# Three graph hops: relation rows from one fp32 one-hot matmul per half group in place of two bf16 ones

## The chip, the core and the metric

One core of one Trainium2 chip. The metric is the device time in microseconds of one execution of the whole program, from one launch; lower is better.

## What is computed

Two graph layers on 6250 nodes with 128 features and 206250 edges (100000 drawn edges, their reverses and one loop per node). The first is an attention layer with two heads. The second, around which the change lies, makes three hops, each over all edges; an edge has one of 64 relations, whose embedding row multiplies the row of its tail node:

```python
head, tail = edge_index            # 206250 edges
rel = edge_emb[edge_type]          # 64 x 128 table, one row per edge
for _ in range(3):
    h, t = agg[head], agg[tail]
    left = h @ q_w
    right = jnp.tanh(rel * t @ k_w)
    att = jnp.sum(left * right, axis=1)
    e = jnp.exp(att - seg_max[head])
    w = e / seg_sum[head]
    summed = segment_sum(w[:, None] * rel * t, head)
    agg = summed / max(cnt, 1);  agg = agg / max(norm(agg), 1e-12)
    out = out + agg + entity_emb
```

## The kernel before

The kernel first sorts the edges by node (until about 830 us of the profile), then runs the attention layer as a pipeline over groups, then the three hops, each again such a pipeline with some bookkeeping between them. A group is 256 edges (`G`), held as two halves of 128. There are 854 groups (`NG`), taken as 61 bodies of 14 (`U`), so the three hops make 2562 groups. The last groups of a pass stand at the end of the sorted list.

There is no scheduler: `pipeline` (line 112) calls one step function per engine and group number k, and in step k each engine works on groups j = k minus a fixed lag, in the written order. Semaphores join the engines. For a hop, the work of one group is:

- POOL (GpSimd), line 705: two indirect DMAs that gather the 128 tail rows of each half into `rows_r`, a ring of 7 groups (`R`). Ahead of them it waits until the group seven back has been multiplied (`val_done`) and its row numbers have been loaded (`peers`).
- SP: once in 7 groups (a unit) it loads for the next unit the target keys (`key_d`, line 461), the small per-group numbers (`meta_d`) and the relation numbers (`type_d`, line 464), keys and relation numbers broadcast to the partitions; for every group the 64 KB tile of `left_d` (line 476); and it stores the finished states (line 483).
- DVE, `masks` (line 1494, lag 4): the one-hot of the relations `hot_r` (line 1503), then the mask of the keys `off_r` (line 1504). At lag 5 line 1655 multiplies the gathered rows with the relation rows out of `bank[0]` into `val_r`. At lag 8 line 1648 takes the running minimum of the scores, and lines 1630 and 1632 accumulate at lag 12.
- PE, in the order of a step: the weighted sums (line 876, lag 11), the transposes of the probabilities (line 882, lag 10), the scores (line 888), the product with `k_w` (line 892), the transposes of `val_r` (line 897, lag 6), and last the relation rows (lines 904 and 905, lag 5). All calls of the helper `mm` show as L737, so its tiles tell them apart: `emb_pair` and `emb_low` for the relation rows, `arena` alone with 128x129 for the sums, `wide` for the scores, `kw_s` for the product.
- ACT: the exponentials (line 1081, lag 9), a count (line 1084), the fade factor (line 1086), and three evacuations of PSUM: line 1090 (probabilities), line 1094 (tanh), line 1098 (`valT`, lag 6).

The relation rows are made exact in bf16 by splitting the fp32 embedding into three bf16 parts. `type_r` holds the relation numbers on all 128 partitions, so `hot_r` has 128 rows: rows 0 to 63 and 64 to 127 are the same one-hot, by `rel_row`. `emb_pair` stacks the high and middle parts, and one matmul over 128 rows adds both; a second, over 64 rows, adds `emb_low`. The parts are prepared once, by nine DVE instructions in `pack` at n == 14, in the sort.

Of the kernel before, what the change touches and what calls it, by code (L numbers as in the profile page):

```python
# [5 lines left out]
P = 128  # L6
N = 6250
E = 206250
F = 128
# [11 lines left out]
R = 7  # L21
# [104 lines left out]
def gnn_kernel(nc, x, src, dst, etype, w, attn_l, attn_r, bias, gamma, beta, emb, q_w, k_w, out):  # L126
    with ExitStack() as ctx:
        ctx.enter_context(nc.allow_non_contiguous_dma(reason="narrow columns of edges and scores"))

        def sb(name, shape, dt=F32):  # L130
            return ctx.enter_context(nc.sbuf_tensor(name, shape, dt))
# [46 lines left out]
        emb_s = sb("emb_s", [2 * RELS, F])  # L178
        emb_rest = sb("emb_rest", [2 * RELS, F])
        emb_high = sb("emb_high", [2 * RELS, F], BF16)  # L180
        emb_pair = sb("emb_pair", [2 * RELS, F], BF16)
        emb_low = sb("emb_low", [RELS, F], BF16)
        rel_row = sb("rel_row", [2 * RELS, 1])
# [95 lines left out]
        hot_r = ring((R, G), BF16)  # L279
# [116 lines left out]
        def _(sp):  # L396
# [18 lines left out]
            for a, d in ((qw_s[:], q_w), (kw_s[:], k_w), (emb_s[0:RELS], emb), (emb_s[RELS:2 * RELS], emb)):  # L415
                sp.dma_start(a, d).then_inc(late_in, 16)
# [21 lines left out]
            def load_store(layer):  # L438
                q = pipes[layer]

                def step(b, k):
# [9 lines left out]
                    if not b.last and k % R == 0 and not (layer == 1 and b.first and k == 0):  # L451
# [11 lines left out]
                        if layer == 1:  # L463
                            sp.dma_start(flat(type_r), row(type_d).partition_broadcast(P)).then_inc(d, 16)
# [21 lines left out]
            def first_unit():  # L486
# [5 lines left out]
                sp.dma_start(flat(type_r), type_d[0:R * G].partition_broadcast(P)).then_inc(d, 16)  # L492
# [242 lines left out]
        def _(pe):  # L735
# [131 lines left out]
            def hop_pe_step(b, k):  # L867
# [32 lines left out]
                if b.has(j):  # L900

                    pe.wait_ge(q["off_done"], b.count(j))
                    for c in range(2):
                        mm(bank[0][:, c * P:(c + 1) * P], hot_r[:, j % R, c * P:(c + 1) * P], emb_pair[:], True, False)
                        last = mm(bank[0][:, c * P:(c + 1) * P], hot_r[0:RELS, j % R, c * P:(c + 1) * P], emb_low[:], False, True)
# [228 lines left out]
        def _(dve):  # L1134
# [79 lines left out]
            def pack(n):  # L1214

                if n == 2:
                    dve.wait_ge(late_in, 10 * 16)
# [15 lines left out]
                elif n == 14:  # L1233
                    do(V.tensor_copy(emb_high[:], emb_s[:]))
                    do(V.tensor_tensor(emb_rest[:], emb_s[:], emb_high[:], ALU.subtract))
                    do(V.tensor_copy(emb_pair[0:RELS], emb_high[0:RELS]))
                    do(V.tensor_copy(emb_pair[RELS:2 * RELS], emb_rest[RELS:2 * RELS]))
                    do(V.tensor_copy(emb_high[0:RELS], emb_rest[0:RELS]))
                    do(V.tensor_tensor(emb_s[0:RELS], emb_rest[0:RELS], emb_high[0:RELS], ALU.subtract))
                    do(V.tensor_copy(emb_low[:], emb_s[0:RELS]))  # L1240
# [490 lines left out]
```

## Time and profile before

| | |
|---|---|
| median of 3 runs | 9809.54 us (9796.19 to 9809.73) |
| the profiled execution, its own time | 9807.02 us |
| span of its trace | 9805.2 us |
| mean granted TensorE clock | 0.979 |
| sort | to about 830 us |
| attention pass, first to last gather | about 830 to 2970 us |
| hop 1, 2, 3: first gather at | 3094, 5332, 7565 us |
| busy share of PE, DVE, ACT, POOL | 91%, 81%, 75%, 69% |

The profile comes from one execution. Engines run side by side, and a busy share is a mean over stages. PE rows give matmuls and PEld rows their weight loads; a matmul overlaps the next one, so the pace of a chain of them is the distance between the starts and not their durations. An fp32 matmul of the program stands as two instructions in the trace, each with a weight load. Time in which an engine waits for nothing that the profile shows is called issue.

### The profile page before, as it was taken

Reading aid. Unit: us, or ns where it says so; the run is one execution under the profiler, and the core shown is the slowest. Engines: PE = TensorE matmul, PEld = TensorE weight load, DVE = VectorE, ACT = ScalarE, POOL = GpSimd, SP = SyncE. Lnnn points to the kernel's source line nnn. Section 1 sums busy time; section 2 is a strip of 40 time slices with the busy share of each in tenths; the row PEclk is TensorE's granted clock in tenths of the full one; section 3 lists DMA queues with packets and bytes.
Section 4 is the critical chain, followed back from the end, with each engine's and each line's share of the span. In section 5 each row is a group of like instructions: output and inputs, shape, how many; then the busy total and the mean of one; then the engine's idle time right before and its main releaser. Section 6 shows DMA issues by size and latency. Waiting matters only on the chain.

```text
span 9805.2 us, 277571 instructions
## 1 busy us (share of the span) xinstructions
PE 8923.7 (91%) x65693; PEld 7235.6 (74%) x65693; DVE 7921.7 (81%) x33650; ACT 7321.4 (75%) x23591; POOL 6810.7 (69%) x7059
## 2 busy tenths in 40 slices
PE   7996777777776999999997999999997999999997
PEld 6985666666664777777775777777775777777775
DVE  7898999999997777777775777777775777777775
ACT  2204999999996777777775777777775777777775
POOL 1336777777775777777775777777775777777775
PEclk9998999999997999999998999999998999999998
DMA  2003444444444555555556555555556555555556
GB/s 49 5 12 82 108 109 109 109 109 109 109 109 115 159 159 159 159 159 158 159 159 133 158 160 160 157 159 159 159 159 140 159 159 159 159 159 159 159 159 122
DMA packets 1133743, 1308.57 MB, mean 133 GB/s; under 512 B 452629, under 2 KB 847723, under 8 KB 1133325
## 3 DMA queue, kind: packets, MB, share of 16 engines
q1 hardware_dynamic: 899446, 841.26, 28.0%
q0 software_dynamic: 229008, 460.45, 21.1%
q10 hardware_dynamic: 5126, 4.76, 0.2%
q8 instruction: 94, 1.54, 0.1%
q14 instruction: 69, 0.56, 0.0%
HBM read 1041.61 MB, written 260.45 MB: 133 GB/s over the span
## 4 chain that ended last, share of the span: by engine, by line
PE 63%; DMA 10%; DVE 9%; issue 8%; POOL 7%; ACT 3%; SPq 1%; DVEq 0%; POOLq 0%; ACTq 0%
PE bank L737 52%; DMA agg<-agg_d,arena 6%; POOL agg L705 6%; PE bank L897 5%; PE bank L882 5%; PE bank L850 2%; DMA agg<-feat_d,arena 2%; DVE agg L1545 2%; DVE agg L1555 2%; ACT arena L1011 2%; DVE arena L1535 1%; POOL wide L718 1%; DMA arena<-type_d 1%; DVE arena L1513 1%; DVE arena L1504 0%
## 5 line engine op out<-in xcount | busy, mean ns | idle before, releaser
L705 POOL DMA_INDIRECT agg<-agg_d,arena x5124 | 4852.1, 947 | 1731.1 <-issue 1432.1
L1655 DVE TENSOR_TENSOR arena<-agg,bank 128x256 f32<-128x256 f32 x2562 | 1080.2, 422 | 1451.1 <-PE bank L737 1064.4
L705 POOL DMA_INDIRECT agg<-feat_d,arena x1708 | 1618.3, 947 | 529.4 <-issue 421.4
L737 PE MATMUL bank<-arena 128*128 128x129 f32 x10248 | 1825.6, 300 | 32.6 <-ACT arena L1090 30.5
L737 PE MATMUL bank<-tmp,wide 128*128 128x256 f32 x5124 | 1540.1, 383 | 10.1 <-DMA wide<-left_d 10.1
L737 PE MATMUL bank<-tmp,kw_s 128*128 128x256 f32 x5124 | 1532.9, 381 | 0.0
L737 PEld LDWEIGHTS bank<-arena 128*128 128x128 f32 x10248 | 1338.5, 190 | 211.3 <-issue 43.3
L1086 ACT ACTIVATE arena<-arena 128x1 f32<-128x1 f32 x2562 | 754.6, 295 | 931.7 <-DVE arena L1519 890.6
L1081 ACT ACTIVATE arena<-agg,arena 128x256 f32<-128x256 f32 x2562 | 1337.9, 522 | 57.8 <-DVE arena L1648 52.2
L1094 ACT ACTIVATE tmp<-bank 128x256 f32<-128x256 f32 x2562 | 982.1, 383 | 427.6 <-PE bank L737 372.6
L1648 DVE CUSTOM_DVE_ANT_0 agg<-bank,arena 128x256 f32<-128x256 f32 x2562 | 1228.6, 480 | 19.6 <-issue 8.0
L737 PE MATMUL bank<-emb_low,arena 64*128 64x128 bf16 x5124 | 1160.3, 226 | 0.0
L737 PE MATMUL bank<-emb_pair,arena 128*128 128x128 bf16 x5124 | 1153.0, 225 | 1.8 <-ACT wide L1002 1.8
L737 PEld LDWEIGHTS bank<-tmp,kw_s 128*128 128x128 f32 x5124 | 979.0, 191 | 134.1
L897 PE MATMUL bank<-ident,arena 128*128 128x128 f32 x5124 | 989.3, 275 | 82.4 <-DVE arena L1655 80.4
L1084 ACT ACTIVATE tmp<-arena 128x256 bf16<-128x256 bf16 x2562 | 1059.9, 414 | 0.0
L1504 DVE TENSOR_SCALAR arena<-arena 128x256 bf16<-128x256 uint16 x3416 | 999.7, 293 | 0.0
L897 PEld LDWEIGHTS bank<-ident,arena 128*128 128x128 f32 x5124 | 715.0, 141 | 373.6 <-DVE arena L1655 125.5
L882 PE MATMUL bank<-ident,arena 128*128 128x128 f32 x5124 | 981.2, 273 | 0.0
L1098 ACT COPY tmp<-bank 128x256 f32<-128x256 f32 x2562 | 942.4, 368 | 17.9 <-PE bank L897 17.5
L850 PE MATMUL bank<-ident,arena 128*128 128x128 f32 x3416 | 561.6, 287 | 425.1 <-ACT arena L1011 423.3
L1513 DVE TENSOR_SCALAR arena<-arena 128x1 f32<-128x1 f32 (+1 forms) x3416 | 930.1, 272 | 0.0
(242 smaller groups left out, 17251.0 us busy)
## 6 DMA issues: line engine op xcount, KB each, us to landing
state_d<-arena SPq DMA_DIRECT2D x488, 455.0 KB, 2.7
arena<-key_d SPq DMA_DIRECT2D x489, 448.0 KB
arena<-type_d SPq DMA_DIRECT2D x367, 448.0 KB
wide<-left_d SPq DMA_DIRECT2D x2562, 64.0 KB
agg<-agg_d,arena POOLq DMA_INDIRECT x5124
agg<-feat_d,arena POOLq DMA_INDIRECT x1708
arena<-er_d SPq DMA_DIRECT2D x854, 1.0 KB
arena<-peers SPq DMA_DIRECT2D x489, 7.0 KB
```

What stands on the lines that cost most here:

```text
L705: nc.gpsimd.indirect_dma_start(out=rows_r[:, k % R, c, 0:width], out_offset=None, in_=table, in_offset=bass.IndirectOffsetOnAxis(ap=peer_r ...
L737: return nc.tensor.matmul(out, lhsT, rhs, start=start, stop=stop)
L882: last = nc.tensor.transpose(bank[4][:, c * P:(c + 1) * P], prob_r[:, j % 2, c * P:(c + 1) * P], ident[:])
L897: last = nc.tensor.transpose(bank[1][:, c * P:(c + 1) * P], val_r[:, j % R, c, 0:F], ident[:])
L1081: nc.scalar.activation(prob_r[:, j % 2, 0:G], score_r[:, j % R, 0:G], ACT.Exp, scale=-1.0, bias=min_r[:, j % R, 0:1]).then_inc(q["exp_done ...
L1084: nc.scalar.activation(nohit_r[:, j % R, :], off_r[:, j % R, :], ACT.Exp, scale=-1.0, accum_out=cnt_r[:, j % R, 0:1])
L1094: nc.scalar.activation(right_r[:, j % R, :], bank[2][:, 0:G], ACT.Tanh).then_inc(q["right_done"], 1)
L1098: nc.scalar.copy(valT_r[:, j % R, :], bank[1][:, 0:G]).then_inc(q["valT_copied"], 1)
L1504: V.tensor_scalar(off_r[:, j % R, :], key_r[:, j % U, :], unit_meta[:, j % U, TARGET:TARGET + 1], BIG, ALU.not_equal, ALU.mult).then_inc(q ...
L1513: V.tensor_scalar(min_in_r[:, j % R, 0:n], min_r[:, (j - 1) % R, 0:n], m[:, KEEP:KEEP + 1], m[:, RESET:RESET + 1], ALU.mult, ALU.add).then ...
L1648: V.tensor_tensor_reduce(out=score_r[:, j % R, 0:G], in0=bank[(3, 7)[j % 2]][:, 0:G], in1=off_r[:, j % R, :], scale=1.0, scalar=min_in_r[: ...
L1655: V.tensor_tensor(val_r[:, j % R, :, 0:F], rows_r[:, j % R, :, 0:F], bank[0][:, 0:G].rearrange("p (c f) -> p c f", c=2), ALU.mult).then_in ...
```

## The change

The one-hot has 64 rows and is fp32, and one fp32 matmul of it with the fp32 embedding gives the relation rows of a half group. `hot_r` becomes a ring of 2 in place of 7, the relation numbers are loaded to 64 partitions in place of 128, and the split of the embedding goes away. In the changed file the lines behind the declarations stand 5 lower in number, and those behind `pack` 16 to 21 lower.

```diff
-        emb_s = sb("emb_s", [2 * RELS, F])
-        emb_rest = sb("emb_rest", [2 * RELS, F])
-        emb_high = sb("emb_high", [2 * RELS, F], BF16)
-        emb_pair = sb("emb_pair", [2 * RELS, F], BF16)
-        emb_low = sb("emb_low", [RELS, F], BF16)
-        rel_row = sb("rel_row", [2 * RELS, 1])
+        emb_s = sb("emb_s", [RELS, F])
...
-        hot_r = ring((R, G), BF16)
+        hot_r = ring((2, G))
...
-                            sp.dma_start(flat(type_r), row(type_d).partition_broadcast(P)).then_inc(d, 16)
+                            sp.dma_start(flat(type_r)[0:RELS], row(type_d).partition_broadcast(RELS)).then_inc(d, 16)
...
                     pe.wait_ge(q["off_done"], b.count(j))
                     for c in range(2):
-                        mm(bank[0][:, c * P:(c + 1) * P], hot_r[:, j % R, c * P:(c + 1) * P], emb_pair[:], True, False)
-                        last = mm(bank[0][:, c * P:(c + 1) * P], hot_r[0:RELS, j % R, c * P:(c + 1) * P], emb_low[:], False, True)
+                        last = mm(bank[0][:, c * P:(c + 1) * P], hot_r[0:RELS, j % 2, c * P:(c + 1) * P], emb_s[:])
                     last.then_inc(q["rel_ready"], 1)
...
-                elif n == 14:
-                    do(V.tensor_copy(emb_high[:], emb_s[:]))
-                    do(V.tensor_tensor(emb_rest[:], emb_s[:], emb_high[:], ALU.subtract))
-                    do(V.tensor_copy(emb_pair[0:RELS], emb_high[0:RELS]))
-                    do(V.tensor_copy(emb_pair[RELS:2 * RELS], emb_rest[RELS:2 * RELS]))
-                    do(V.tensor_copy(emb_high[0:RELS], emb_rest[0:RELS]))
-                    do(V.tensor_tensor(emb_s[0:RELS], emb_rest[0:RELS], emb_high[0:RELS], ALU.subtract))
-                    do(V.tensor_copy(emb_low[:], emb_s[0:RELS]))
-                    do(V.tensor_scalar(rel_row[:], rowid[:, 0:1], RELS - 0.5, -float(RELS), ALU.is_ge, ALU.mult))
-                    do(V.tensor_tensor(rel_row[:], rel_row[:], rowid[:, 0:1], ALU.add))
...
-                    V.tensor_scalar(hot_r[:, j % R, :], type_r[:, j % U, :], rel_row[:, 0:1], None, ALU.is_equal)
+                    V.tensor_scalar(hot_r[0:RELS, j % 2, :], type_r[0:RELS, j % U, :], rowid[0:RELS, 0:1], None, ALU.is_equal)
```

On PE, the end of one step of a hop and the start of the next stand so before (`kw_s` is the product, `ident,arena` at L897 the transposes of `val_r`, `arena` with 128x129 the sums):

```order
L737 MATMUL bank<-tmp,kw_s 128x256
L897 MATMUL bank<-ident,arena 128x128 x2
L902 REGISTER_ALU
L737 MATMUL bank<-emb_pair,arena 128x128
L737 MATMUL bank<-emb_low,arena 128x128
L737 MATMUL bank<-emb_pair,arena 128x128
L737 MATMUL bank<-emb_low,arena 128x128
```

and so in the changed program, where `mm` is line 732:

```order
L732 MATMUL bank<-tmp,kw_s 128x256
L892 MATMUL bank<-ident,arena 128x128 x2
L897 REGISTER_ALU
L732 MATMUL bank<-emb_s,arena 128x128 x2
L732 MATMUL bank<-arena 128x129 x2
```

Four bf16 matmuls became two fp32 ones (four instructions in a trace) at the same place, between the transposes of `val_r` and the sums of the next step.

## Rows read from the trace of the kernel before

**Rows 1.** The page: busy time, share of the span and instructions of each engine.

```profile
PE 8923.7 (91%) x65693; PEld 7235.6 (74%) x65693; DVE 7921.7 (81%) x33650; ACT 7321.4 (75%) x23591; POOL 6810.7 (69%) x7059
```

**Rows 2.** Windows in attention pass, hop 1: us, busy of PE PEld DVE ACT POOL, PEclk, DMA, GB/s.

```profile
900.00:2900.00 2000.00, 1569.40 (x12810) 1367.62 (x12810) 1951.55 (x8119) 1835.77 (x4803) 1511.45 (x1600) 1.00 0.43 109
3200.00:5150.00 1950.00, 1938.14 (x12464) 1533.58 (x12463) 1512.81 (x7123) 1549.20 (x5453) 1475.05 (x1559) 1.00 0.55 159
```

**Rows 3.** Groups of POOL: attention pass (900:2900), then hop 1 (3200:5150).

```profile
L705 POOL DMA_INDIRECT agg<-feat_d,arena x1600 | 1511.8, 945 | 488.8 <-issue 388.8 <-PE bank L737 100.0
L705 POOL DMA_INDIRECT agg<-agg_d,arena x1559 | 1476.0, 947 | 475.3 <-issue 395.1 <-DVE arena L1655 80.2
```

**Rows 4.** Waits of POOL in hop 1 (3200:5150): us in total, times, longest.

```profile
POOL agg L705 <- DVE arena L1655: 80.2, 263, 0.3
```

**Rows 5.** Timeline of PE, one group of hop 2: start us, us, engine, line, instruction.

```profile
5503.23 0.38 PE L897 MATMUL bank<-ident,arena 128*128 128x128 f32 x2
5503.45 0.22 PE L737 MATMUL bank<-emb_pair,arena 128*128 128x128 bf16 x1
5504.08 0.71 PE L737 MATMUL bank<-arena 128*128 128x129 f32 x4
5504.63 0.38 PE L882 MATMUL bank<-ident,arena 128*128 128x128 f32 x2
5505.93 0.22 PE L737 MATMUL bank<-emb_pair,arena 128*128 128x128 bf16 x1
```

**Rows 6.** Groups of the hops by form: weight loads of the sums and of the relation rows.

```profile
L737 PEld LDWEIGHTS bank<-arena 128*128 128x128 f32 x10248 | 1338.5, 190 | 211.3 <-issue 43.3 <-DVE arena L1632 6.2
L737 PEld LDWEIGHTS bank<-emb_pair,arena 128*128 128x128 bf16 x5124 | 497.8, 97 | 173.2 <-issue 2.3
```

**Rows 7.** Timeline of ACT and PEld in the same group.

```profile
5503.71 0.37 ACT L1098 COPY tmp<-bank 128x256 f32<-128x256 f32 x1
5503.97 0.52 ACT L1081 ACTIVATE arena<-agg,arena 128x256 f32<-128x256 f32 x1
5504.52 0.25 PEld L882 LDWEIGHTS bank<-ident,arena 128*128 128x128 f32 x2
```

**Rows 8.** DVE: timeline of the same group, then one group row of hop 1 (3200:5150).

```profile
5502.74 0.28 DVE L1503 TENSOR_SCALAR arena<-arena,rel_row 128x256 bf16<-128x256 uint16 x1
5502.93 0.28 DVE L1504 TENSOR_SCALAR arena<-arena 128x256 bf16<-128x256 uint16 x1
5503.15 0.48 DVE L1648 CUSTOM_DVE_ANT_0 agg<-bank,arena 128x256 f32<-128x256 f32 x1
...
L1655 DVE TENSOR_TENSOR arena<-agg,bank 128x256 f32<-128x256 f32 x779 | 328.4, 422 | 422.5 <-PE bank L737 322.6 <-DMA agg<-agg_d,arena 97.9 <-issue 1.6
```

**Rows 9.** The ends of hops 1, 2 and 3: chain, then DVE's timeline.

```profile
5229.47 17.81 DMA arena<-type_d
...
5247.31 0.18 DVE L1501 COPY arena<-arena 128x28 f32<-128x28 f32 x1 [14.08 <-DMA arena<-type_d]
...
5248.19 0.42 DVE L1655 TENSOR_TENSOR arena<-agg,bank 128x256 f32<-128x256 f32 x1
...
5267.11 0.42 DVE L1655 TENSOR_TENSOR arena<-agg,bank 128x256 f32<-128x256 f32 x1 [0.55 <-PE bank L737]
...
7496.69 0.42 DVE L1655 TENSOR_TENSOR arena<-agg,bank 128x256 f32<-128x256 f32 x1 [1.57 <-DMA agg<-agg_d,arena]
...
9720.19 0.18 DVE L1501 COPY arena<-arena 128x28 f32<-128x28 f32 x1 [16.24 <-DMA arena<-type_d]
```

**Rows 10.** A window of 10 us at the end of hop 1, columns as in rows 2.

```profile
5220.00:5230.00 10.00, 7.63 (x46) 5.18 (x45) 5.16 (x25) 4.48 (x18) 0.00 (x0) 1.00 0.95 35
```

**Rows 11.** Timeline of the sort around the split of the embedding.

```profile
164.35 0.22 DVE L1234 CAST emb_high<-emb_s 128x128 bf16<-128x128 f32 x1
166.75 0.89 DVE L1414 TENSOR_TENSOR arena<-bank,arena 128x343 f32<-128x343 f32 x2
168.42 0.10 PEld L737 LDWEIGHTS bank<-arena,before 128*128 128x128 bf16 x1 [0.21 <-DVE arena L1382]
```

More of the change, by code:

```diff
@@ L414, in _ @@
             sp.dma_start(sorted_edges[1][NB * REGION:NB * REGION + G].rearrange("(l w) o -> l (w o)", l=1), zeros[0:1, :]).then_inc(prefilled, 16)
-            for a, d in ((qw_s[:], q_w), (kw_s[:], k_w), (emb_s[0:RELS], emb), (emb_s[RELS:2 * RELS], emb)):
+            for a, d in ((qw_s[:], q_w), (kw_s[:], k_w), (emb_s[:], emb)):
                 sp.dma_start(a, d).then_inc(late_in, 16)
@@ L491, in first_unit @@
                 sp.dma_start(flat(unit_meta), meta_d[1].rearrange("p g c -> p (g c)")[:, 0:R * MW]).then_inc(d, 16)
-                sp.dma_start(flat(type_r), type_d[0:R * G].partition_broadcast(P)).then_inc(d, 16)
+                sp.dma_start(flat(type_r)[0:RELS], type_d[0:R * G].partition_broadcast(RELS)).then_inc(d, 16)
             def load_states(layer):
@@ L1216, in pack @@
                 if n == 2:
-                    dve.wait_ge(late_in, 10 * 16)
+                    dve.wait_ge(late_in, 9 * 16)
                     do(V.tensor_tensor(shifted_i.bitcast(F32), shifted_i, dst_i, ALU.is_lt))
```

## The prediction

> **What bounds the kernel now.** I read the page first: PE is busiest, at 91% [rows 1], and the change takes work from PE, so the first thought is that PE's gain is the kernel's gain. The windows ask whether that holds where the change acts. In the hops PE is busy 1938 of 1950 us, POOL only 1475 [rows 2]. But POOL's gap between two gathers is no idle time that something could fill: the groups of POOL show 947 ns for a gather and 475.3 / 1559 = 0.305 us ahead of each, of which most ends in "issue", with nothing waited for [rows 3]. So a gather takes 1.252 us and a group, with two, 2.504 us.
>
> The test is the attention pass. There PE is busy 1569 of 2000 us, so it has a fifth of its time to spare, at a granted clock of 1.00 [rows 2], and the gathers come at the same pace: 945 ns and 488.8 / 1600 = 0.306 us, 1.251 us each [rows 3]. A pace that is the same beside a full and beside a slack PE is POOL's own. The gaps that are put down to DVE's line 1655 say it again: 80.2 us in 263 times [rows 4] is 0.305 us each, exactly the length of the issue gap. The wait ended before the gap did, and cost nothing.
>
> PE's own pace is the distance between two starts of the relation rows: 5505.93 - 5503.45 = 2.48 us [rows 5]. So two engines run side by side, POOL at 2.50 and PE at 2.48 us a group. POOL is the bound by 0.02 us, and PE is full only because it follows it closely. From the first gather to the last, 3 hops of 854 groups at 2.50 make 6400 of the 9807 us.
>
> **The change, part by part.** The sum is made against the profiled execution's own 9807.0 us (span 9805.2), which is 2.5 us below the median of 9809.5.
>
> *Relation rows on PE.* Before, four bf16 instructions take 5504.08 - 5503.45 = 0.63 us from the first one's start to the sums [rows 5]. After, there are four fp32 instructions of 128 columns. The nearest row is the sums: four fp32 instructions of 129 columns, each with its own weight load, 5504.63 - 5504.08 = 0.55 us. Lower end: the fp32 transposes, two in 5503.45 - 5503.23 = 0.22 us, so 0.44 for four [rows 5]. Upper end: four loads one behind the other at 190 ns [rows 6], 0.76 us. I take 0.55, as the sums have the same kind of instruction and a load each. PE's work per group goes from 2.48 to 2.40 us (2.29 to 2.61).
>
> The trace shows that an fp32 load is twice as long as a bf16 one, 190 against 97 ns, and that four of the former are nonetheless hidden within 0.55 us [rows 5, 6]. The Trainium skill, page "TensorE: Matmul & The Clock Gate", section "Weight-path perf modes — Fast Weight Load (FWL) and DoubleRow", speaks against this change: the fast weight load applies to full-width weights only when they are not fp32, so the new matmuls give it up; if that load were exposed the sum would be that of the first rival below, and by the row of the sums it is not.
>
> *What this is worth.* Up to the point where PE needs 2.50, nothing in the steady part: 2562 groups x 0. What is late next is already late: the gather. What remains of PE's gain lies where PE catches up, at the end of a hop. There DVE's line 1655 runs 8 times between 5248.19 and 5267.11 [rows 9], nearly all behind PE, so at most 3 x 8 x 0.08 = 1.9 us. Against even that stands a ring. The transposes of `val_r` start at 5503.23, ACT's copy of them at 5503.71, its exponential at 5503.97, ending at 5504.49, and the loads for the transposes of the probabilities start at 5504.52 [rows 5, 7]. Those transposes run at 5504.63, and the next transposes of `val_r`, one period behind the last, at 5505.71. The ring is 2.48 us long with 0.03 us to spare, and none of it gets shorter: what the relation rows give up becomes a wait for ACT. I take -1 us, between 0 and -1.9.
>
> *The one-hot on DVE.* It now writes fp32 on 64 partitions. The old one takes 0.19 us up to the next instruction [rows 8]. Bounds: 0.19 (nothing changes) and the 0.42 of line 1655, an fp32 instruction of the same 256 columns. I take 0.30, between them since only the output changes width. DVE waits 422.5 / 779 = 0.54 us per group ahead of line 1655 [rows 8], so +0.11 (0 to +0.23) is covered; were that cover gone it would cost 2562 x 0.11 = 280 us. ACT's exponential needs line 1648, which ends at 5503.63, 0.34 us ahead of its start at 5503.97 [rows 7, 8]; that cover holds at both ends too. 0 us.
>
> *Ring of 2 in place of 7.* No wait is added. DVE writes the one-hot of group j in step j+4; in step j+3 it has waited, ahead of line 1655, for the relation rows of group j-2, whose slot this is. 0 us.
>
> *Half the relation load.* 448 KB become 224 KB once in 7 groups. In the steady part DMA is busy 0.55 [rows 2] and nobody waits for it. At the end of a hop it is different: the share is 0.95 at 35 GB/s, and POOL does not gather at all for a while [rows 10]. There SP's loads queue up among slow gather packets, and `type_d`, the last of the unit's three, is what DVE waits for: 17.81 us from issue to landing, 14.08 us of wait in hop 1 and 16.24 in hop 3 [rows 9]. From there PE's 2.48 us steps run to the end of the hop, so an earlier landing counts in full. Bounds: 0, if the keys ahead of it on the queue hold it up, and a third of the 17.81 us, 6 us, if the time goes by the packets of this load among its neighbours (the keys are as large, `left_d` and the state store share the queue). I take 1.5 us in each of hops 1 and 3, near the lower end, since the keys and small numbers go first and keep their size, and nothing in hop 2, where line 1655 waited at the end, at 7496.69, for gathers [rows 9]: -3 us (0 to -18).
>
> *Setup.* The nine DVE instructions lie between 164.35 and 166.75, 2.4 us, but PE, which sets the pace there, idles only 0.21 us [rows 11]: -0.2 us. The second load of the embedding goes too, 0.
>
> Sum: -1 - 3 - 0.2 = -4 us, **9803 us**.
>
> **Rivals.**
> *PE becomes the bound (slower).* Price: if the loads are not hidden, four of 190 ns [rows 6] make 0.76 us, PE's group 2.61, and 2562 x (2.61 - 2.504) = +272 us: 10079. It decides from 0.65 us for the four, since 1.85 us of PE's step is other work and 0.65 fills it to 2.50. For it: only 0.10 us lie between that point and my 0.55, and no row shows fp32 weights on 64 rows. Against: the sums [rows 5] carry the same four loads. 7%.
>
> *The gathers slow down with DVE (slower).* If POOL's work waited for the longer one-hot each time, 2562 x 0.11 = +280 us: 10087. The Trainium skill, "GPSIMD Engine Reference", section "1. Specifications", says that GpSimd shares its SBUF interfaces with VectorE and contends with some of its instructions. Against: DVE is busy 1951 of 2000 us in the attention pass and 1513 of 1950 in the hops, and a gather takes 945 and 947 ns [rows 2, 3]. 3%.
>
> *PE's gain counts after all (faster).* If the gathers' pace hung on PE, the group would follow PE to 2.40: -0.08 x 2562 = -205 us, 9602, and at 0.44 for the four instructions -487, 9320. Against: the attention pass. 5%.
>
> *The tail gets more (faster).* `type_d` lands 6 us earlier in all three hops: -18 us and -2 of catching up, 9787. For it: the load is on the chain. Against: the end of hop 2 hung on gathers, and a hop that ends earlier meets that limit. 11%, half of it beyond 0.2%.
>
> *No change on the path at all*, 9807, is within the forecast.
>
> **How the numbers follow.** About 0.2% (20 us) is what a measurement of this kernel can tell from no change; the three runs shown lie 13.5 us apart. Forecast, within 0.2%: 74%; with half of the tail's rival that makes 79% same. Faster: 5 + 5.5, about 11%. Slower: 7 + 3, 10%. The range holds the forecast, the tail's rival, and the spread of runs: 9786 (9807 less 21) to 9824 (a run at the top of the spread, with some 14 us for a hop's end that falls worse among the slow packets). It leaves out the PE rivals of both signs and the slower gathers, 15%.
>
> **What the profile would show.** Right: gathers at 947 ns and 0.305 us in the hops; the four new instructions 0.55 us from first to next; PE idle of about 0.1 us a group appearing ahead of line 877 or the transposes of `val_r`; the one-hot row longer, DVE's wait for PE of 0.54 us shorter or equal; moved bytes down by 367 x 224 KB = 84 MB; `type_d` still the wait that ends last in hop 3's end. Wrong: a group period under 2.49 us in the hops (then POOL was not the bound), or over 2.52 with gaps ahead of the gathers longer than 0.31 us that DVE's line for `val_r` ends (then PE is).

## The result, and the profile after

The changed kernel takes 9980.24 us (median of 4 runs, 9973.47 to 9989.28) against 9804.75 us (median of 4, 9796.19 to 9809.73): a ratio of 1.0184, with a 95% interval of 1.0171 to 1.0196. It is slower by 175 us. The forecast was 9803 with a range of 9786 to 9824, so both the number and the sign were wrong. The profiled execution took 9973.47 us, with a span of 9971.6, which is 166.4 more than the span of before.

The page (busy time and share of each engine, then DMA), to be set beside [rows 1]:

```profile
PE 9161.3 (92%) x65693; PEld 7681.5 (77%) x65693; DVE 8041.6 (81%) x33641; ACT 7371.7 (74%) x23591; POOL 6920.2 (69%) x7059
...
DMA packets 1110172, 1224.34 MB, mean 123 GB/s; under 512 B 452612, under 2 KB 847642, under 8 KB 1109756
```

The page alone says little: PE has the same number of instructions and 238 us more of busy time, POOL 110 more. The windows (busy us of PE, PEld, DVE, ACT, POOL, then granted clock, DMA share, GB/s) say where, beside [rows 2]:

```profile
900.00:2900.00 2000.00, 1570.32 (x12809) 1368.19 (x12807) 1951.79 (x8123) 1837.57 (x4805) 1511.42 (x1601) 1.00 0.43 109
3200.00:5150.00 1950.00, 1950.00 (x12079) 1617.47 (x12078) 1501.86 (x6902) 1515.51 (x5285) 1468.81 (x1515) 1.00 0.53 142
```

The attention pass is what it was. In hop 1 PE is now busy 1950 of 1950 us at the full granted clock, and does less in it: POOL issues 1515 gathers where it issued 1559, which makes 1950 / 1515 x 2 = 2.574 us a group in place of 2.50. From the first gather to the last the three hops take 2219.1, 2217.2 and 2219.3 us; before, 2156.6, 2155.0 and 2158.5. Together that is +185.5 us, more than the whole difference. The rest gives some back: the first gather of hop 1 comes at 3090.2 in place of 3094.0 us, and the ends of the hops and what lies between them are 15 us shorter.

The timeline of PE over one group of hop 2 (start, duration, engine, line, instruction), beside [rows 5]:

```profile
5561.27 0.38 PE L892 MATMUL bank<-ident,arena 128*128 128x128 f32 x2
5561.58 0.71 PE L732 MATMUL bank<-emb_s,arena 64*128 64x128 f32 x4
5562.22 0.71 PE L732 MATMUL bank<-arena 128*128 128x129 f32 x4
5562.77 0.38 PE L877 MATMUL bank<-ident,arena 128*128 128x128 f32 x2
...
5563.85 0.38 PE L892 MATMUL bank<-ident,arena 128*128 128x128 f32 x2
5564.16 0.71 PE L732 MATMUL bank<-emb_s,arena 64*128 64x128 f32 x4
```

From one group's relation rows to the next is 5564.16 - 5561.58 = 2.58 us. The steps around them, before and after: transposes to relation rows 0.22 and 0.31, relation rows to sums 0.63 and 0.64, sums to the transposes of the probabilities 0.55 and 0.55. With the 0.09 that is lost ahead of them, the four new matmuls cost 0.73 us, not 0.55. And 1.85 us of other work and 0.73 make the 2.58.

The timeline of the weight loads at that place shows what is odd about them:

```profile
5561.58 0.52 PEld L732 LDWEIGHTS bank<-emb_s,arena 64*128 64x128 f32 x4 [0.17 <-issue]
5562.22 0.52 PEld L732 LDWEIGHTS bank<-arena 128*128 128x128 f32 x4
5562.66 0.25 PEld L877 LDWEIGHTS bank<-ident,arena 128*128 128x128 f32 x2
```

The loads of the transposes begin at 5562.66, 0.11 us ahead of their matmul at 5562.77. The loads of the relation rows and those of the sums begin at 5561.58 and 5562.22, together with their matmuls, and ahead of the former the load path stands idle for 0.17 us. These are the two places where weights of 64 rows follow weights of 128, or the other way round.

Groups of DVE and POOL in hop 1 (3200 to 5150 us: count, busy us, mean ns, then idle time ahead and what ended it), beside [rows 3, 8]:

```profile
L1639 DVE TENSOR_TENSOR arena<-agg,bank 128x256 f32<-128x256 f32 x755 | 319.2, 423 | 434.4 <-PE bank L732 384.5 <-issue 49.9
L1487 DVE TENSOR_SCALAR arena<-arena,rowid 64x256 f32<-64x256 uint16 x755 | 257.3, 341 | 0.0
```

```profile
L700 POOL DMA_INDIRECT agg<-agg_d,arena x1515 | 1469.2, 970 | 481.3 <-issue 469.4 <-DVE arena L1639 11.9
```

DVE's multiplication waited 97.9 us of this stretch for gathered rows before; now 384.5 and 49.9 are the whole of its 434.4, and none is left for them. The rows are always there, and what it waits for is PE. That is the row that names the bound.

POOL, though, is not far behind it, and its row is a warning: its gathers are longer, 970 ns against 947, and it waits little where one can see it. Left to itself it would take 2 x (0.970 + 0.305) = 2.55 us a group, only 0.03 under PE's 2.58. Were the longer gathers the bound, DVE would use the rows soon after they come. The trace shows the reverse: the last gather of a group ends 6.9 us ahead of DVE's multiplication of its rows at 3250 us, and 13.3 us ahead at 4700 us (in the kernel before 4.8 and 3.7 us). POOL runs ahead of PE, slowly, until the ring of 7 groups is full.

### The profile page after: what moved, and what is told of

The parts are those of the page before. It is cut to its first block, busy times and chain, and to the rows that moved or that the text cites. A ratio compares the mean times of both kernels' runs of the same rounds, so it can differ in the third digit from the quotient of the medians.

```text
span 9971.6 us, 277561 instructions
## 1 busy us (share of the span) xinstructions
PE 9161.3 (92%) x65693; PEld 7681.5 (77%) x65693; DVE 8041.6 (81%) x33641; ACT 7371.7 (74%) x23591; POOL 6920.2 (69%) x7059
## 2 busy tenths in 40 slices
DMA packets 1110172, 1224.34 MB, mean 123 GB/s; under 512 B 452612, under 2 KB 847642, under 8 KB 1109756
## 4 chain that ended last, share of the span: by engine, by line
PE 76%; DVE 7%; issue 5%; POOL 5%; DMA 5%; ACT 2%; DVEq 0%; SPq 0%; POOLq 0%; ACTq 0%
PE bank L732 62%; PE bank L892 6%; PE bank L877 5%; POOL agg L700 4%; DMA agg<-feat_d,arena 2%; PE bank L845 2%; DVE agg L1539 1%; DVE agg L1529 1%; ACT arena L1005 1%; DMA agg<-agg_d,arena 1%; DVE arena L1519 1%; POOL wide L713 1%; DMA arena<-peers 1%; DVE arena L1497 0%; PE bank L837 0%
## 5 line engine op out<-in xcount | busy, mean ns | idle before, releaser
L700 POOL DMA_INDIRECT agg<-agg_d,arena x5124 | 4960.3, 968 | 1807.9 <-issue 1711.4
L732 PE MATMUL bank<-emb_s,arena 64*128 64x128 f32 x10248 | 1824.6, 298 | 1.8 <-ACT wide L996 1.8
L732 PEld LDWEIGHTS bank<-emb_s,arena 64*128 64x128 f32 x10248 | 1332.3, 187 | 433.7 <-issue 331.2
L1632 DVE CUSTOM_DVE_ANT_0 agg<-bank,arena 128x256 f32<-128x256 f32 x2562 | 1203.7, 470 | 12.2 <-issue 6.4
L1488 DVE TENSOR_SCALAR arena<-arena 128x256 bf16<-128x256 uint16 x3416 | 948.2, 278 | 0.0
```

The costliest lines, as they stand in the source:

```text
L700: nc.gpsimd.indirect_dma_start(out=rows_r[:, k % R, c, 0:width], out_offset=None, in_=table, in_offset=bass.IndirectOffsetOnAxis(ap=peer_r ...
L732: return nc.tensor.matmul(out, lhsT, rhs, start=start, stop=stop)
L1488: V.tensor_scalar(off_r[:, j % R, :], key_r[:, j % U, :], unit_meta[:, j % U, TARGET:TARGET + 1], BIG, ALU.not_equal, ALU.mult).then_inc(q ...
L1632: V.tensor_tensor_reduce(out=score_r[:, j % R, 0:G], in0=bank[(3, 7)[j % 2]][:, 0:G], in1=off_r[:, j % R, :], scale=1.0, scalar=min_in_r[: ...
```

## The experiments

Theory A: each change between weights of 64 and of 128 rows costs about 0.2 us of PE's time, and after has two of them a group. Theory B: fp32 matmuls of a one-hot cost this whatever their rows. Theory C: DVE's longer one-hot or the ring of 2 holds the group. Beside them stands the prediction's ring of 2.48 us, by which PE could not be faster than that whatever the relation rows cost. Theories D (slack on PE costs clock, and thereby time) and E (the fp32 one-hot on DVE lengthens the gathers) came up on the way.

| run | us | against before |
|---|---|---|
| after | 9980.2 | 1.0184 [1.0171, 1.0196] |
| rows128_again | 9833.6 | 1.0032 [1.0021, 1.0043] |
| rows128_load64_again | 9831.6 | 1.0029 [1.0018, 1.0040] |
| low128_again | 9815.8 | 1.0014 [1.0005, 1.0023] |
| low128_fill | 9803.7 | 1.0001 [0.9992, 1.0010] |
| extra_f32 | 9833.9 | 1.0035 [1.0022, 1.0048] |
| split_switch_again | 10842.0 | one run |
| before_half | 9651.2 | one run, half the gathers |
| rows128_half | 8956.2 | one run, half the gathers |

### On a slower chip

**rows128**: after, with weights of 128 rows. The embedding is padded with 64 rows of zeros.

```diff
-        emb_s = sb("emb_s", [RELS, F])
+        emb_s = sb("emb_s", [2 * RELS, F])
...
-                            sp.dma_start(flat(type_r)[0:RELS], row(type_d).partition_broadcast(RELS)).then_inc(d, 16)
+                            sp.dma_start(flat(type_r), row(type_d).partition_broadcast(P)).then_inc(d, 16)
...
-                        last = mm(bank[0][:, c * P:(c + 1) * P], hot_r[0:RELS, j % 2, c * P:(c + 1) * P], emb_s[:])
+                        last = mm(bank[0][:, c * P:(c + 1) * P], hot_r[:, j % 2, c * P:(c + 1) * P], emb_s[:])
...
+                elif n == 14:
+                    do(V.memset(emb_s[RELS:2 * RELS], 0.0))
...
-                    V.tensor_scalar(hot_r[0:RELS, j % 2, :], type_r[0:RELS, j % U, :], rowid[0:RELS, 0:1], None, ALU.is_equal)
+                    V.tensor_scalar(hot_r[:, j % 2, :], type_r[:, j % U, :], rowid[:, 0:1], None, ALU.is_equal)
```

> The changed kernel with a one-hot of 128 rows (rows 64 to 127 never match, the embedding has zeros there) and the relation numbers loaded to 128 partitions again: no 64-row weights are left. Theory A (each change between 64-row and 128-row weights stops the load-ahead and exposes one fp32 load, two such changes a group, 0.2 us each): PE's work falls from 2.58 to about 2.18 us a group, the relation rows take 0.44 us and the sums 0.44, POOL's 2.50 is the bound again and the time is that of the kernel before, 9805 us within 20. Theory B (fp32 matmuls of a one-hot cost this, whatever the rows): PE stays at 2.58 us a group and the time at about 9980. Theory C (DVE's longer one-hot or the ring of 2 holds the group): 9980 too, with gaps on PE.

**rows128_load64**: the same, with the load of the relation numbers left at 64 partitions as in after (what stands in the other 64 meets rows of zeros).

```diff
-                            sp.dma_start(flat(type_r), row(type_d).partition_broadcast(P)).then_inc(d, 16)
+                            sp.dma_start(flat(type_r)[0:RELS], row(type_d).partition_broadcast(RELS)).then_inc(d, 16)
```

> As rows128, but the relation numbers are loaded to 64 partitions as in the change (the other 64 hold what is there, and multiply zeros). Against rows128 it tells what half the load is worth. The prediction's term: 3 us earlier, 0 to 18. By theory A about 9800 to 9805 us; by B and C about 9975.

**low128**: before, with the third bf16 part padded to 128 rows.

```diff
-        emb_low = sb("emb_low", [RELS, F], BF16)
+        emb_low = sb("emb_low", [2 * RELS, F], BF16)
...
-                        last = mm(bank[0][:, c * P:(c + 1) * P], hot_r[0:RELS, j % R, c * P:(c + 1) * P], emb_low[:], False, True)
+                        last = mm(bank[0][:, c * P:(c + 1) * P], hot_r[:, j % R, c * P:(c + 1) * P], emb_low[:], False, True)
...
-                    do(V.tensor_copy(emb_low[:], emb_s[0:RELS]))
+                    do(V.tensor_copy(emb_low[0:RELS], emb_s[0:RELS]))
+                    do(V.memset(emb_low[RELS:2 * RELS], 0.0))
```

> The kernel before, with the third bf16 part padded by zeros to 128 rows and its matmul over all 128 rows of the one-hot: four bf16 matmuls, no 64-row weights. Theory A: the four changes of row count a group go; the four instructions take 0.25 to 0.45 us in place of 0.63 and the sums behind them 0.44 in place of 0.55, so PE has 2.1 to 2.3 us of work; POOL is the bound before and after, so the time stays within 20 us of 9805, perhaps a few us less at the ends of the hops. Theory B: PE's rows stay as they were, and so does the time. If PE bound the kernel before after all, the time falls by 0.2 x 2562 = 500 us or more.

**split_switch**: after, with the relation rows of half 0 ahead of the transposes of `val_r` and those of half 1 behind them. The same instructions, with four changes of the row count a group in place of two.

```diff
+                if b.has(k - 5):
+                    pe.wait_ge(q["off_done"], b.count(k - 5))
+                    relation(k - 5, 0)
                 if b.has(j):
...
-                    for c in range(2):
-                        last = mm(bank[0][:, c * P:(c + 1) * P], hot_r[0:RELS, j % 2, c * P:(c + 1) * P], emb_s[:])
-                    last.then_inc(q["rel_ready"], 1)
+                if b.has(k - 5):
+                    relation(k - 5, 1).then_inc(q["rel_ready"], 1)
```

> The changed kernel with the relation rows of half 0 ahead of the two transposes of the values and those of half 1 behind them: the same instructions, but four changes of row count a group in place of two. Theory A: 2 x 0.2 us more on PE, 2.98 us a group, about 10980 to 11010 us. Theory B and C: 2.58 us a group and about 9980 us.

Measured: 13149.6 (ratio 0.9971 [0.9960, 0.9983]), 13148.1 (0.9972), 13162.6 (0.9981 [0.9971, 0.9991]) and 13406.2 us. On this chip before itself takes 13184.5 us (13167 to 13199, 17 runs). The four expectations named times between 9800 and 11010 us, so none came true. In the trace of rows128 PE is busy only 74% of the span, and DVE's multiplication stands idle for 3223.0 us in the hops, 2565.9 of them ended by something that is none of this core's engines; that these are gathered rows that land late is the likely reading, and not shown. So none of the four numbers can be set against the 9980: most of PE's work is covered there. Only split_switch, whose PE is the slowest of all, comes through, +222 us in its one run. All four were run again on a chip where before takes 9801.9 us, below.

### With half the gathers: what PE does alone

To see PE's own pace, POOL must be out of the way. Both kernels here leave out the gather of the second half of every group in the hops.

```diff
-                {"peers": (U, 16), "unit": (U, 48), "block": (U, 16), "gathered": (R, 32), "stored": (U, 16)}]
+                {"peers": (U, 16), "unit": (U, 48), "block": (U, 16), "gathered": (R, 16), "stored": (U, 16)}]
...
-                    for c in range(2):
+                    for c in range(2 - layer):
```

**before_half** is before with that edit:

> The kernel before, with only the first half of each group's gathers in the three hops (the second half of the rows is left out and holds old data): POOL needs 1.25 us a group. It asks what PE and ACT allow when the gathers don't bound the hops. If POOL's 2.50 was the bound and PE's 2.48 close behind, PE now sets 2.48 us a group and the time falls only by 60 us, and some tens more at the ends of the hops, where half of the slow gathers go: 9680 to 9745 us on a chip where the kernel before takes 9805. If the gathers were not the bound, no change in the inner part.

**rows128_half** is rows128 with it:

> The same with the 128-row fp32 one-hot, whose work on PE is 2.18 us a group by theory A. If the ring that the prediction named (value transposes, ACT's copy, ACT's exponential, probability transposes) is 2.48 us long whatever the relation rows cost, this takes as long as before_half. If there is no such ring, PE sets 2.18 us a group and it is 0.3 x 2562 = 770 us faster than before_half. By theory B PE is at 2.58 and it is 250 us slower than before_half.

Measured: 9651.2 and 8956.2 us. The windows and the POOL group of before_half, 3200 to 4800 us:

```profile
3200.00:4800.00 1600.00, 1600.00 (x10324) 1272.47 (x10323) 1257.30 (x5897) 1291.89 (x4518) 613.76 (x646) 1.00 0.45 134
...
L705 POOL DMA_INDIRECT agg<-agg_d,arena x646 | 614.6, 951 | 987.6 <-DVE arena L1655 911.4 <-issue 76.1
```

And of rows128_half:

```profile
3200.00:4800.00 1600.00, 1600.00 (x11627) 1489.69 (x11626) 1444.22 (x6643) 1456.30 (x5088) 722.41 (x728) 1.00 0.50 151
...
L700 POOL DMA_INDIRECT agg<-agg_d,arena x728 | 724.3, 995 | 878.8 <-DVE arena L1641 783.8 <-issue 95.0
```

In both, PE is busy all the time and POOL waits for room in the ring of gathered rows: 911.4 / 646 = 1.41 and 783.8 / 728 = 1.08 us ahead of each gather, put down to DVE's multiplication that frees a place. This is how a POOL that is held up looks. With one gather a group, 646 and 728 of them in 1600 us are 2.48 and 2.20 us a group. So PE's own step was 2.48 us before, as the prediction read it, and with fp32 weights of 128 rows it is 2.20. **The ring of 2.48 us falls**: had it held PE, the two would be equally long. They differ by 695 us; 770 were expected, and the two paces make 2562 x 0.28 = 717. **Theory B falls** too, as by it rows128_half would be 250 us slower than before_half. before_half itself came out 29 us under its expected range: the steady pace accounts for 2562 x (2.504 - 2.477) = 69 of the 153 us that it gains, and the other 84 were not followed. The transposes, copy, exponential and next transposes that the prediction joined to a ring can evidently run 0.28 us closer. How they do was not followed further.

### The same edits where the gathers are fast

**rows128_again** and **rows128_load64_again**:

> rows128 again, since its first run met a chip on which the kernel before itself takes 13185 us and where the gathers' landing, not their pace, sets the group. Where the kernel before takes 9805: theory A, PE at 2.18 us a group under POOL's 2.50, so the time of the kernel before within 20 us, likely 5 to 20 us less at the hops' ends, as PE catches up faster (rows128_half has shown no ring of 2.48 us); theories B and C, about 9980.

> rows128_load64 again, for the same reason. Against rows128_again it is the worth of half the relation load: the prediction's term says 3 us less, 0 to 18. By theory A about 9780 to 9800 us.

Measured: 9833.6 us (9832.55 to 9841.98) and 9831.6. PE's timeline of rows128_again in hop 2:

```profile
5559.54 0.61 PE L732 MATMUL bank<-emb_s,arena 128*128 128x128 f32 x4
5559.98 0.61 PE L732 MATMUL bank<-arena 128*128 128x129 f32 x4
5560.43 0.38 PE L877 MATMUL bank<-ident,arena 128*128 128x128 f32 x2
...
5561.51 0.38 PE L892 MATMUL bank<-ident,arena 128*128 128x128 f32 x2
5561.73 0.61 PE L732 MATMUL bank<-emb_s,arena 128*128 128x128 f32 x4
```

The three distances that made the difference read 0.22 (transposes to relation rows), 0.44 (relation rows) and 0.45 us (sums), where after has 0.31, 0.64 and 0.55. The step is 5561.73 - 5559.54 = 2.19 us, so 0.39 of after's 2.58 belong to the row count alone: the same instructions on the same columns, DVE's one-hot on 128 partitions in place of 64 (359 ns against 341), the weights padded with zeros. The weights and the one-hot that streams past them change their rows together in every run here, so no run tells which of the two counts. The records of the single matmuls, which the rows above fold into groups, place it: at a change the first matmul starts 0.20 us after the one ahead of it and the second 0.21 us after the first, where all others of 128 columns start 0.11 us apart. Padding takes back 147 of the 175 us. **Theory C falls**: the fp32 one-hot and the ring of 2 are still there. But theory A's time was missed: within 20 us of before, likely 5 to 20 less, was expected, and it is 32 us more, and 30 with the half load (9780 to 9800 expected).

The half load is worth 2.0 us between these two, within their intervals, so nothing that could be told from zero. The missing 30 us come up again below.

**split_switch_again**, four changes a group:

> split_switch again, for the same reason. Its first run showed on PE the stops that theory A names, each at 0.20 us in place of 0.11, with the next interval 0.21. Here they should set the time: 2.98 us a group and 10980 to 11010 us. Theories B and C: about 9980.

Measured: 10842.0 us. PE's timeline, hop 2:

```profile
6000.98 0.71 PE L732 MATMUL bank<-arena 128*128 128x129 f32 x4
...
6002.70 0.48 PE L732 MATMUL bank<-emb_s,arena 64*128 64x128 f32 x2
6003.12 0.44 PE L899 MATMUL bank<-ident,arena 128*128 128x128 f32 x2
6003.49 0.48 PE L732 MATMUL bank<-emb_s,arena 64*128 64x128 f32 x2
6003.90 0.71 PE L732 MATMUL bank<-arena 128*128 128x129 f32 x4
```

6003.90 - 6000.98 = 2.92 us. With none, two and four changes PE's step is 2.19, 2.58 and 2.92 us: 0.195 us for each of the first two and 0.17 for each of the others. That is somewhat under what theory A said for four (2.98), and 10842 us lies under its 10980 to 11010. Of the two added changes one goes to the relation rows and costs 0.195 again; the other goes to the transposes, whose loads are shorter (142 ns a load on the page of after, against 187 for the relation rows), and costs 0.15 (the single records start 0.20 and 0.165 us apart there, in place of 0.11 and 0.11). Together 0.345, measured 0.34. So a change costs about one load of the weights behind it. Nothing was added but the order, and it cost 862 us, in one run. **Theory A holds**, in sign and place, and in size once the length of the load is counted.

**low128_again**, the change's counterpart in bf16:

> low128 again, for the same reason. Its first run showed the four bf16 matmuls 0.056 us apart. Theory A: PE has about 2.0 us of work a group, POOL's 2.50 stays the bound, and the time is that of rows128_again within 10 us, 0 to 25 us under the kernel before.

Measured: 9815.8 us. PE's timeline, hop 1:

```profile
3254.63 0.22 PE L737 MATMUL bank<-emb_pair,arena 128*128 128x128 bf16 x1
3254.68 0.22 PE L737 MATMUL bank<-emb_low,arena 128*128 128x128 bf16 x1
...
3254.85 0.66 PE L737 MATMUL bank<-arena 128*128 128x129 f32 x4
3255.35 0.38 PE L882 MATMUL bank<-ident,arena 128*128 128x128 f32 x2
```

Four bf16 matmuls over 128 rows take 0.22 us, where before they alternate between 128 and 64 rows and take 0.63 [rows 5]. So the old kernel paid for its changes too, four a group and inside the very 0.63 us that the change was measured against; and the sums take 0.50 here, not 0.55. In bf16 a change costs 0.16 - 0.056 = 0.10 us, again about one load (92 to 97 ns in before). PE's step falls by 0.46 us, to 2.02, and the kernel does not get faster: POOL holds it at 2.50. It even gets slower than before, by 14 us, where 0 to 25 less was expected, and it is 18 us faster than rows128_again, where 10 at most was expected. That was a new question.

### What slack on PE costs

The windows of low128_again, and the timeline of PE ahead of the second of them:

```profile
3200.00:5150.00 1950.00, 1714.26 (x12419) 1497.41 (x12418) 1491.88 (x7099) 1518.12 (x5435) 1476.12 (x1555) 0.96 0.55 158
3240.00:3249.00 9.00, 4.92 (x34) 3.73 (x32) 3.52 (x18) 3.50 (x14) 6.87 (x8) 0.98 0.71 212
3249.00:3252.00 3.00, 2.76 (x13) 2.34 (x11) 2.25 (x12) 2.38 (x9) 2.12 (x3) 0.50 0.17 46
3252.00:3260.00 8.00, 8.00 (x65) 7.37 (x64) 6.96 (x33) 7.20 (x25) 6.12 (x7) 1.00 0.56 158
```

```profile
3248.39 0.52 PE L897 MATMUL bank<-ident,arena 128*128 128x128 f32 x2 [3.06 <-DVE arena L1656]
```

PE stands still for 3.06 us (DVE ahead of it waits for gathered rows), and the granted clock falls to 0.50, the lower level of 1.2 GHz, for the next 3 us; then it is 1.00 again. Over the stretch of 1950 us the clock is 0.96, which is 2 x 0.04 x 1950 = 156 us at the lower level. Before and after have 1.00 there: a PE without slack has no such pauses. Theory D says that these cost the 14 us. To test it, **low128_fill** gives PE something to do: the four matmuls are issued three times, and only the last round counts.

```diff
-                    for c in range(2):
+                    for c in (0, 1) * 3:
```

> low128 with its group of four bf16 matmuls issued three times (the last one counts, the result is the same), which adds 8 x 0.056 = 0.45 us to PE, 2.42 us a group, still under POOL's 2.50. low128_again, with about 1.97 us of work on PE, was 14 us slower than the kernel before, with the clock at 0.96 to 0.97 in the inner part of the hops, where it is 1.00 in the kernel before. Theory D (PE that has caught up stands still when gathers land late, the clock falls for a while, and POOL then waits for the values): with little slack left PE rarely stands long, the clock is back at 1.00, and the time is that of the kernel before within 10 us. If the 14 us have another cause, it stays at 9815.

```profile
3200.00:5150.00 1950.00, 1939.54 (x18716) 1800.41 (x18715) 1502.84 (x7131) 1552.44 (x5458) 1475.00 (x1559) 1.00 0.55 159
```

Measured: 9803.7 us, 12 us less than low128_again and with a clock of 1.00; half as many more instructions on PE in this window, and they cost no time. It ties with before (1.0001 [0.9992, 1.0010]) and does not beat it. The slowest of the 11 runs of low128_fill (9813.1) is still under the fastest of the 10 of low128_again (9814.8). That slack on PE costs 12 us here, and that filling it gives them back, is shown. Whether the clock does it or PE's idling itself is not, as filling changes both. By which way it reaches POOL is not shown either: POOL waits no more in low128_again than before. Its gathers are longer, in the POOL groups of both in the same window (low128_again, then low128_fill):

```profile
L705 POOL DMA_INDIRECT agg<-agg_d,arena x1555 | 1476.7, 950 | 474.0 <-issue 419.4 <-DVE arena L1656 54.3 <-DMA arena<-peers 0.3
```

```profile
L705 POOL DMA_INDIRECT agg<-agg_d,arena x1559 | 1476.3, 947 | 475.3 <-issue 397.6 <-DVE arena L1656 77.7
```

3 ns on 5124 gathers are 15 us, the size of the loss.

### What the fp32 one-hot costs beside the gathers

rows128_again is 18 us slower than low128_again, with a higher clock in this window (0.98 against 0.96), and its gathers take 954 ns against 950:

```profile
L700 POOL DMA_INDIRECT agg<-agg_d,arena x1550 | 1478.4, 954 | 472.6 <-issue 420.7 <-DVE arena L1641 51.8
```

Theory E is the prediction's second rival. **extra_f32** is before with one more DVE instruction, which writes the same one-hot in fp32 into a spare ring that nobody reads.

```diff
+        spare_hot = sb("spare_hot", [P, 2, G])
...
+                    V.tensor_scalar(spare_hot[:, j % 2, :], type_r[:, j % U, :], rel_row[:, 0:1], None, ALU.is_equal)
```

> The kernel before with one more instruction of DVE a group: the same one-hot also written as fp32 over 128 partitions into a spare buffer that nobody reads. PE's work is unchanged. Theory E (the gathers get longer where DVE writes the wide one-hot, as 947 became 970 ns in the changed kernel and 954 in rows128_again): a gather's mean rises from 947 to 955 to 970 ns, and with POOL the bound the time rises by 2 x 2562 x 8 to 23 ns = 40 to 120 us. If DVE doesn't touch the gathers, 947 ns stays and the time is that of the kernel before within 20 us, since DVE has 0.54 us a group to spare.

The groups of extra_f32 in hop 1, DVE's new instruction and the gathers:

```profile
L1505 DVE TENSOR_SCALAR spare_hot<-arena,rel_row 128x256 f32<-128x256 uint16 x776 | 282.0, 363 | 0.0
```

```profile
L706 POOL DMA_INDIRECT agg<-agg_d,arena x1552 | 1477.9, 952 | 473.2 <-issue 411.0 <-DVE arena L1657 62.2
```

Measured: 9833.9 us, +32 us (1.0035 [1.0022, 1.0048]), less than the 40 to 120 expected, and a gather longer by 5 ns where 8 to 23 were. The clock is 1.00 in this window, so it is not theory D. The gathers take 952 ns in place of 947, and 5 ns x 5124 = 26 us is most of it. So DVE's work can reach POOL, by nanoseconds. Whether it is the fp32 output or only one instruction more stays open, as no kernel with the same instruction in bf16 was run.

## Why the prediction was wrong, and where it was right

**The step that failed** is "I take 0.55, as the sums have the same kind of instruction and a load each". The four measure 0.73 us (0.09 lost ahead of them and 0.64), so PE's group is 2.58 us where the prediction had 2.40, and PE passes POOL's 2.50. The nearest row differed from the new instructions in one thing besides a column, the 64 rows of the weights, and that was the thing that mattered: with 128 rows they would have taken 0.44, with 64 they bring two changes of the row count at 0.195 each. What is more, the row was itself no clean one: the same sums take 0.45 us where nothing changes ahead of them (rows128_again), and 0.50 behind bf16 weights of 128 rows (low128_again). The 0.55 held a change already, and the prediction read it as four hidden loads.

The trace of before could have warned. Four bf16 matmuls took 0.63 us where four fp32 instructions of the same width take 0.44 by the row of the transposes, and the prediction never asked what was so slow in the 0.63. A row that it did not show, the loads of the third bf16 part in the hops by form, before:

```profile
L737 PEld LDWEIGHTS bank<-emb_low,arena 64*128 64x128 bf16 x5124 | 472.0, 92 | 576.1 <-issue 404.9
```

The load path stood idle for 576.1 / 5124 = 0.11 us ahead of each of these, mostly in "issue", and for 173.2 / 5124 = 0.03 us ahead of those of 128 rows beside them [rows 6]. A shape that makes the load path idle was there to be seen, with the 64 rows on it.

**The rule that was weighed.** The prediction held the Trainium skill, page "TensorE: Matmul & The Clock Gate", section "Weight-path perf modes — Fast Weight Load (FWL) and DoubleRow", against the row of the sums, and set it aside. For weights that keep their row count the runs agree: in rows128_again the fp32 loads take 195 ns each and are fully hidden, at 0.44 us for four. At a change of the row count they don't: there one load is exposed, and the fp32 one is twice as long. So PE's step without any change rises from 2.02 to 2.19 us, and the changes cost 0.39 us, two in fp32, in place of 0.46, four in bf16: together 0.10 more, the 2.58 against 2.48. Whether the fast path is what makes the bf16 load short, no run here shows.

**The deciding point was right, its price nearly so, its chance far too small.** The first rival, PE as the bound, was said to decide from 0.65 us; the real 0.73 is above it, and PE's group is 2.58 us where that rival said 2.61. Its +272 would have been 2562 x (2.58 - 2.504) = +195 by the real duration; +185.5 was measured between first and last gathers, and +166.4 in all. Its mechanism, all four loads exposed, was wrong: one load at each of the two places of change is. The prediction's sign of this rival came true by half: the period is over 2.52, but of the gaps ahead of the gathers (481.3 / 1515 = 0.318 us) DVE's line ends only 11.9 us in all, as POOL with its longer gathers is itself at 2.55. A rival 0.10 us from the forecast, on an instruction shape that no row showed, was worth more than 7%.

**POOL as the floor at 2.50 was right.** rows128_again has 0.29 us less of PE work a group than before, low128_again 0.46 less, and neither is faster. That also answers the third rival: PE's gain does not count. When half of the gathers are left out, before gains 153 us, and rows128 877 (9833.6 - 8956.2).

**The ring of 2.48 us was wrong**, as rows128_half shows. It had no part in the sum beyond the choice of -1 us, but it made the forecast feel safe. Instructions that follow one another closely in one period are no ring unless something makes each of them wait.

**DVE's one-hot**: 0.26 us up to the next instruction (0.30 taken), and its time on DVE is covered as said. Not covered is what it does to the gathers: the prediction's second rival is there at a small size, 32 us by extra_f32 and 18 by rows128_again against low128_again, not 280. In after the gathers are 23 ns longer; no one waits for them, but they put POOL's own floor at 2.55 us in place of 2.50.

**The ring of 2** adds no wait, as said. **The half load**: 84 MB fewer are moved (1308.57 to 1224.34 MB), as said, and it is worth 2 us against the -3 taken, and no part of it is certain. DVE's waits for `type_d` in after are no proof to the contrary:

```profile
5280.56 0.18 DVE L1485 COPY arena<-arena 128x28 f32<-128x28 f32 x1 [14.88 <-DMA arena<-type_d]
```

They add up to 39.8 us against 56.6 before, but to 47.9 in rows128_again with the full load and 56.8 in rows128_load64_again with the half one. The ends of the hops scatter by this much. **Setup**: hop 1 begins 3.8 us earlier, against the -0.2 taken; which part is the sort's was not followed.

## What to carry to other kernels

In a tight chain on TensorE, keep one row count for all weights, and pad the narrower ones with zeros: the rows are free (0.44 us for four with 128 of them), and the change of the count is not (0.2 us each in fp32, 0.1 in bf16). That pays only where TensorE is the bound: here no padded kernel beat before. When a cost is taken from the nearest row, list in what the new instruction differs from it, and ask what the row's own neighbours have put into it; price a rival by how near the deciding point lies, not by how clean the forecast's story is. And when an engine that is not the bound gets lighter, expect nothing, or slightly less than nothing.

## What was not expected of the hardware

- **Weight loads run ahead only while the row count stays.** fp32 matmuls of 128 columns start 0.11 us apart; at a change between 64 and 128 rows the first starts 0.20 and the second 0.21 us after the one ahead. For bf16 it is 0.056 against 0.16 us. The price of a change follows the load: 0.195 us for loads of 187 to 190 ns, 0.15 for 142 ns, 0.10 for 92 to 97 ns. The Trainium skill, page "TensorE: Matmul & The Clock Gate", section "The mechanism", says that "LDWEIGHTS overlaps with in-flight MATMULs only when row_grp differs". These traces do not bear out the sentence: the loads run ahead where the rows are the same 128, and stop where their number differs. Read by its letter, rows128 would have been the slow one. The same section also lets a load run ahead when it goes to a background weight buffer, which would allow the loads on the same rows; of what a change of the row count does it says nothing.
- **The granted clock depends on pauses, not on the share alone.** In the attention pass PE is busy 78% of the time and the clock is 1.00 [rows 2]; in hop 1 of low128_again it is busy 88% and the clock is 0.96, at the lower level after pauses such as the 3.06 us above.
- **A gather's own length moves** by a few ns with what other engines do: 947 (before and low128_fill), 950 (low128_again), 952 (extra_f32), 954 (rows128_again), 970 (after), and 995 in rows128_half. The Trainium skill, "GPSIMD Engine Reference", section "1. Specifications", tells of contention between GpSimd and VectorE over shared interfaces; extra_f32 agrees in sign, with 5 ns a gather, though the page names DVE instructions with two SBUF inputs or in a two-port mode, and no run here tells in which mode the added one ran. What makes 970 of it in after was not tried by itself; split_switch_again has 966.
- **The same program takes 9802 us on one chip and 13184 on another**, and the two rank the same kernels differently: rows128 is at 1.0032 of before on the one and 0.9971 on the other. Late gathered rows are the likely cause; no trace of before on the second chip was kept.
